# Score maxima of an attention kernel from 28-row bands: two heads by a quarter of the keys in a tile

## The chip, the cores and the metric

One core of one Trainium2 chip. The metric is device time in microseconds (us) of one execution of the whole program; lower is better.

## What is computed

Layer norm of x (2048 rows by 256), cross attention onto a context of 1601 rows with 8 heads of dimension 4, a gated residual, a second layer norm, then a router with 8 experts that each take their 512 best rows:

```
q, k, v = heads(ln(x) @ Wq + bq), heads(ctx @ Wk + bk), heads(ctx @ Wv + bv)
attn = softmax(q @ k.T * scale)              # per head, 2048 x 1601
x = x + tanh(g_x) * (attn @ v @ Wo + bo)
scores = softmax(ln(x) @ router_w + router_b); G, idx = top_k(scores.T, 512)
h1 = relu(toks @ w1 + b1); eo = (h1 @ w2 + b2) * G
x = x + tanh(g_f) * scatter_add(eo, idx)
```

The change is in the attention alone: in how the row maximum of the scores, which the softmax subtracts, is found.

## The kernel before

**Data.** Each number of q and k is split into bf16 parts, so that a head takes 28 rows (partitions) of contraction at most: 6 groups of 4 for the products of the parts, of which rows 24 and 25 also carry the maximum. Four heads stand under each other, head hh at partitions 32·hh to 32·hh+27. qrows holds q in that form (2 groups of 4 heads). kpad (L141) holds k once for each head, with all partitions but the head's own set to zero (L807 and L590 multiply by a 0/1 column), so that a matmul over all 128 partitions gives the scores of one head.

**Units.** The queries go in 4 chunks of 512, times 2 groups of 4 heads: 8 units, numbered u = 0 to 7. A unit has 13 steps (kt), one for each tile of 128 keys (the last has 65). In a step TensorE does, for each head hh of the group:

- a score matmul (L1287, called S here), 128 keys by 512 queries, into bank hh mod 2. It waits until ScalarE has read what was there before, two heads earlier (L1284).
- ScalarE's exponential of it (L609), which writes probs in fp32.
- after the second S of a step, the product of the step before with the values (L1191, called P here): 4 heads, 4 column groups of the array, fp32, 8 records.

**The maximum.** It has to be known before a unit's scores are taken. So it is found one unit ahead, two steps early (LEAD, L295): max_scores (L1165, called M here) makes a tile of two 401-column matmuls (L1175) of 128 queries against kpad, in two neighbouring banks; VectorE reduces the tile (max_half, L811 to L814). Before, both matmuls of a tile are of one head with one stationary block of q, and the tile is that head's half of the keys. A unit has 32 tiles (HALVES, L43). halves_of (L297) spreads them over the steps: 3 in steps 0, 2, 4, 6, 8 and 10 of a unit, 2 in the other seven. On TensorE the order of a step is S M S (M) P S M S, where (M) is there in steps of 3 tiles only. Unit 0's 32 tiles and the first 4 of unit 1 (EARLY, L301) stand ahead of all steps. Unit 7 computes no maxima. max_parts (L816) takes the maximum over a head's tiles, place_max (L1178) and q_full bring it into rows 24 and 25 of qfull.

**Side jobs.** At the end of some steps, behind the fourth S, stands a job of TensorE for a neighbouring chunk (L314 and on): transposes (L1199, L1132, L1206, L1220, L1232), place_max (L1181), the output projection (wo, L1210 to L1214), the q projection (L1138), the router (L1226).

**Loops.** All engines write chunk 0 and chunk 3 out and run chunks 1 and 2 in a loop with a register (on TensorE L1328, ScalarE L655, VectorE L941).

Of the kernel before, what the change touches and what calls it, by code (L numbers as in the profile page):

```python
# [13 lines left out]
ALU = mybir.AluOpType  # L14
ACT = mybir.ActivationFunctionType
AX = mybir.AxisListType

P = 128
# [12 lines left out]
NC = 4  # L31
CT = QT // NC
CW = CT * P
# [3 lines left out]
HG = 4  # L37
# [2 lines left out]
NKB = len(KB) * NG  # L40
MAXW = 401
MAXSTEP = 400
HALVES = CT * HG * 2  # L43
ROW_V = 28
KROW_M = 24
BITS = 30
# [50 lines left out]
def build(nc, x, ctxt, g_x, g_f, Wq, bq, Wk, bk, Wv, bv, Wo, bo, rw, rb, w1, b1, w2, b2, cf, cdigits, out, x2d):  # L97
# [9 lines left out]
    with es:  # L107
# [3 lines left out]
        def sem(name):  # L111
            return es.enter_context(nc.semaphore(name))
# [25 lines left out]
        def ar(name, shape, dt=F32):  # L138
            return arena.enter_context(nc.sbuf_tensor(name, shape, dt))

        kpad = ar("kpad", [P, NH, KEYS], BF16)  # L141
        vp = ar("vp", [P, NKT, NG, HG, 32])
        qrows = ar("qrows", [P, NG, S], BF16)
# [10 lines left out]
        rec = ar("rec", [P, CT, HG])  # L154
        on = ar("on", [P, CT, NG, HG, HD])
        mparts = ar("mparts", [P, CT, HG, 32], BF16)
        mhalf = ar("mhalf", [P, HALVES])
        nmax = ar("nmax", [P, CT * HG])
        wq_sb = ar("wq_sb", [P, KD, 32])
        wk_sb = ar("wk_sb", [P, KD, 32])  # L160
# [74 lines left out]
        ps = es.enter_context(nc.psum_tensor("ps", [P, 8, 512], F32))  # L235
# [18 lines left out]
        s_mm, s_mr, s_nm, s_mhi, s_mp, s_mpl, s_qf = [sem(n) for n in ("max_scores", "max_reduced", "max_negated", "max_high", "max_parts", "max_placed", "q_full")]  # L254
# [19 lines left out]
        s_dn, s_bi, s_eo, s_put = sem("down_steps"), sem("b2_added"), sem("expert_out"), sem("rows_added")  # L274

        block = es.enter_context(nc.Block())

        def kt_rows(kt):
            return P if kt < FULLKT else KREST
# [20 lines left out]

        EARLY = HALVES * LEAD // NKT  # L301
        PLACE = NKT - LEAD
# [399 lines left out]
        def _(dve):  # L702
# [12 lines left out]
            for w, r in ((wk_sb, wkr), (wq_sb, wqr)):  # L715
                for k in range(KD):
                    for g in range(NG):
                        last = nc.vector.tensor_copy(
                            r[:, k, g, :].rearrange("p (h j d) -> p h j d", h=HG, d=HD)[:, :, 0:6, :],
                            w[:, k, 16 * g:16 * g + 16].rearrange("p (h d) -> p h d", d=HD).unsqueeze(2).to_broadcast([P, HG, 6, HD]))  # L720
# [7 lines left out]
            for j in range(2):  # L728
                for g in range(NG):
                    last = nc.vector.tensor_copy(  # L730
                        bqkr[:, NG * j + g, :].rearrange("p (h j d) -> p h j d", h=HG, d=HD)[:, :, 0:6, :],
                        bias_sb[:, 32 * j + 16 * g:32 * j + 16 * g + 16].rearrange("p (h d) -> p h d", d=HD).unsqueeze(2).to_broadcast([1, HG, 6, HD]))
# [67 lines left out]
            for j in range(4):  # L800
                lo, w = KB[j]
# [3 lines left out]
                for hh in range(HG):  # L805
                    last = nc.vector.tensor_scalar(kpad[:, hh, lo:lo + w], krows[:, 0:w],
                                                   cst[:, C_HEAD + hh:C_HEAD + hh + 1], None, ALU.mult)  # L807
# [3 lines left out]
            def max_half(u, j):  # L811
                dve.wait_ge(s_mm, HALVES * u + j + 1)
                b = 2 + 2 * (j % 2)
                nc.vector.tensor_reduce(mhalf[:, j:j + 1], ps[:, b:b + 2, 0:MAXW], AX.XY, ALU.max).then_inc(s_mr, 1)  # L814

            def max_parts(u):  # L816

                dve.wait_ge(s_mr, HALVES * (u + 1))
                nc.vector.tensor_reduce(nmax[:, :], mhalf[:, :].rearrange("p (n h) -> p n h", h=2), AX.X, ALU.max,
                                        negate=True).then_inc(s_nm, 1)  # L820
                dve.wait_ge(s_nm, u + 1)
                at_least(dve, s_mpl, u)
                nm = nmax[:, :].rearrange("p (t h) -> p t h", h=HG)
                nc.vector.tensor_copy(mparts[:, :, :, KROW_M], nm).then_inc(s_mhi, 1)
                dve.wait_ge(s_mhi, u + 1)
                nc.vector.tensor_tensor(mparts[:, :, :, KROW_M + 1], nm, mparts[:, :, :, KROW_M], ALU.subtract).then_inc(s_mp, 1)
# [117 lines left out]
            c = NC - 1  # L944
# [130 lines left out]
            for e in range(E):  # L1075
                for f in range(NF):
                    n = NF * e + f
# [16 lines left out]
                for t in range(NT):  # L1094
                    dve.wait_ge(s_dn, DOWN * e + STEPS_F + 2 * (t // 2) + 2)
                    at_least(dve, s_eo, NT * (e - 1) + t + 1)
                    a = D * (t % 2)
# [4 lines left out]
        def _(pe):  # L1102
            mm = nc.tensor.matmul

            pe.wait_ge(s_wrep, 1)
            for j in range(2 * NG):
                last = mm(job[:, j:j + 1], bqkr[:, j, :], cst[0:1, C_ONE:C_ONE + 1], start=True, stop=True)
# [33 lines left out]
            for j in range(4):  # L1141
                for k in range(KD):
                    n = KD * j + k
                    pe.wait_ge(s_ctx[j], 16)
                    at_least(pe, s_ctt, n - 3)
                    for t in range(4 if j < 3 else 1):
                        w = kt_rows(4 * j + t)
                        last = nc.tensor.transpose(ps[:, n % 4, P * t:P * t + w], ctx_sb[0:w, 4 * j + t, P * k:P * k + P],
                                                   cst[0:w, C_ID:C_ID + w])
# [14 lines left out]

            def max_scores(u, c, g, j):  # L1165

                t, hh, half = j // (2 * HG), (j // 2) % HG, j % 2
                if j == 0:

                    pe.wait_ge(s_rows, ROWS_OF_UNIT[u] if isinstance(u, int) and u < 2 else NKB + u + 1)  # L1170
                at_least(pe, s_mr, HALVES * u + j - 1)
                q = qrows[:, g, bass.ds(CW * c + P * t, P)]
                for b in range(2):
                    lo = MAXSTEP * (2 * half + b)
                    last = mm(ps[:, 2 + 2 * (j % 2) + b, 0:MAXW], q, kpad[:, HG * g + hh, lo:lo + MAXW], start=True, stop=True)  # L1175
                last.then_inc(s_mm, 1)

            def place_max(u):  # L1178
# [146 lines left out]
                return owner[0]  # L1325

            chunk(0, True, False)
            with pe.Fori(1, NC - 1) as i:  # L1328
                chunk(i, False, False)
            owner = chunk(NC - 1, False, True)  # L1330
            c = NC - 1
# [77 lines left out]
            for e in range(E):  # L1409
                for f in range(NF):  # L1410
# [3 lines left out]
                    if f >= LAG:  # L1414
# [3 lines left out]
                        for t in range(NT):  # L1418
                            last = down(e, f - LAG, t)
# [5 lines left out]
                for t in range(NT):  # L1425
                    for f in range(NF - LAG, NF):
                        last = down(e, f, t)
# [21 lines left out]
```

## Time and profile before

| | |
|---|---|
| median of 3 runs | 698.83 us (698.7 to 701.12) |
| the profiled execution | 701.08 us; its span, from the first to the last instruction, 699.3 us |
| mean granted TensorE clock | 0.933 of full speed |
| busy: TensorE matmul, VectorE, ScalarE, GpSimd | 588.2, 479.8, 405.2, 160.4 us |
| projections and unit 0's maxima | to about 75 us |
| the steps of units 0 to 6, with maxima beside them | about 75 to 379 us |
| the steps of unit 7, without | about 379 to 414 us |
| router, search of the thresholds | to about 487 us |
| experts | to the end |

Engine names in the rows: PE is TensorE's matmul, PEld its weight load, DVE is VectorE, ACT is ScalarE, POOL is GpSimd. "128\*32" behind a matmul is rows by columns of the array that it uses. The duration of a PE record is longer than the time for which it holds the next one up: records overlap, so the distance between two starts is what a matmul costs.

### The profile page before, as it was taken

To read this page: it belongs to the slowest core of one execution; us is meant where nothing else is said; L and a number is where in the kernel's file an instruction comes from. 1 tells how busy PE (TensorE), PEld (TensorE's weight loads), DVE (VectorE), ACT (ScalarE), POOL (GpSimd) and SP (SyncE) were. 2 spreads that over 40 slices of the span, in tenths; PEclk is the share of its full clock that TensorE was granted. 3 is DMA by queue.
4 is the path that set the end of the run, shared out by engine and by line. 5 is a ranking of instruction groups with operands and counts; after the bars stand their busy time and mean duration, and the time that the engine had idled before them with its cause. 6 is when DMAs were issued, how large, how long until landed. Compare 5 with 4: busy or idle time off the path is not lost.

```text
span 699.3 us, 10376 instructions
## 1 busy us (share of the span) xinstructions
PE 588.2 (84%) x3452; PEld 318.1 (45%) x3452; DVE 479.8 (69%) x952; ACT 405.2 (58%) x748; POOL 160.4 (23%) x161
## 2 busy tenths in 40 slices
PE   4875899999999999999999983012999999999992
PEld 4421233323333234332332231002889888988991
DVE  3789977779788797886877014885576786786531
ACT  2554478767778677877677961000555666565551
POOL 3023202002030020560000001003143653463333
PEclk9989899999999999999999995555999999999997
DMA  7500000000000000000001005001135554463322
GB/s 249 185 1 0 1 1 0 2 1 1 1 31 31 1 0 0 30 30 0 1 1 60 1 1 180 0 0 38 53 100 141 121 135 126 103 172 100 61 31 30
DMA packets 23326, 35.39 MB, mean 51 GB/s; under 512 B 3411, under 2 KB 15988, under 8 KB 23156
## 3 DMA queue, kind: packets, MB, share of 16 engines
q1 hardware_dynamic: 17140, 26.45, 11.5%
q0 software_dynamic: 6144, 8.39, 7.1%
q8 instruction: 24, 0.39, 0.2%
q14 instruction: 18, 0.15, 0.1%
HBM read 26.45 MB, written 8.39 MB: 50 GB/s over the span
## 4 chain that ended last, share of the span: by engine, by line
PE 71%; DVE 11%; ACT 7%; issue 4%; POOL 2%; DMA 0%; POOLq 0%; DVEq 0%; ACTq 0%
PE ps L1191 14%; PE ps L1392 13%; PE ps L1399 13%; PE ps L1287 13%; PE ps L1175 9%; ACT probs L609 5%; DVE mhalf L814 4%; DVE ge L988 3%; PE ps L1138 2%; PE ps L1214 1%; PE ps L1226 1%; PE ps L1374 1%; PE ps L1115 1%; PE ps L1220 1%; ACT c L540 1%
## 5 line engine op out<-in xcount | busy, mean ns | idle before, releaser
L814 DVE TENSOR_REDUCE mhalf<-ps 128x1 f32<-128x802 f32 x256 | 247.5, 988 | 62.9 <-PE ps L1175 60.4
L609 ACT ACTIVATE probs<-ps 128x512 f32<-128x512 f32 (+1 forms) x416 | 233.1, 599 | 91.0 <-PE ps L1287 88.5
L1287 PE MATMUL ps<-qfull,kpad 128*128 128x512 bf16 (+1 forms) x416 | 153.0, 384 | 7.5 <-ACT probs L609 2.0
L1175 PE MATMUL ps<-kpad,qrows 128*128 128x401 bf16 x512 | 132.8, 343 | 13.2 <-DVE mhalf L814 11.7
L1191 PE MATMUL ps<-probs,vp 128*32 128x512 f32 (+1 forms) x832 | 110.8, 604 | 1.5 <-ACT osb L529 0.9
L1287 PEld LDWEIGHTS ps<-qfull,kpad 128*128 128x128 bf16 (+1 forms) x416 | 40.1, 99 | 141.2 <-ACT probs L609 120.9
L1079 DVE TENSOR_TENSOR h1l<-hf,h1h 128x512 fp32r<-128x512 f32 x64 | 44.5, 695 | 62.3 <-ACT hf L689 54.6
L688 ACT ACTIVATE h1h<-ps,b1T 128x512 fp32r<-128x512 f32 x64 | 43.9, 686 | 60.6 <-PE ps L1392 60.4
L1399 PE MATMUL ps<-w2h,h1h 128*128 128x256 f32 x256 | 73.8, 288 | 3.3 <-issue 2.6
L1175 PEld LDWEIGHTS ps<-kpad,qrows 128*128 128x128 bf16 (+1 forms) x512 | 46.2, 99 | 59.0 <-DVE mhalf L814 27.2
L1399 PE MATMUL ps<-w2l,h1h 128*128 128x256 f32 x256 | 72.4, 283 | 0.0
L1399 PE MATMUL ps<-w2h,h1l 128*128 128x256 f32 x256 | 72.3, 282 | 0.0
L499 POOL DMA_INDIRECT out<-eo,idx_put x32 | 56.9, 1777 | 29.3 <-ACT eo L698 20.2
L413 POOL TENSOR_SCALAR rstd<-mv 128x4 f32<-128x4 f32 x8 | 1.9, 232 | 229.5 <-DVE mv L750 229.5
L1392 PE MATMUL ps<-tokh,w1h 128*128 128x512 f32 x128 | 52.5, 410 | 1.5 <-DVE tokl L1065 1.5
L1399 PEld LDWEIGHTS ps<-w2h,h1h 128*128 128x128 f32 x256 | 48.8, 191 | 7.8 <-issue 5.8
L1392 PE MATMUL ps<-tokl,w1h 128*128 128x512 f32 x128 | 51.1, 399 | 0.0
L1392 PE MATMUL ps<-tokh,w1l 128*128 128x512 f32 x128 | 50.6, 395 | 0.0
L1399 PEld LDWEIGHTS ps<-w2l,h1h 128*128 128x128 f32 x256 | 48.9, 191 | 1.2
L1399 PEld LDWEIGHTS ps<-w2h,h1l 128*128 128x128 f32 x256 | 48.9, 191 | 0.0
L689 ACT ACTIVATE hf<-ps,b1T 128x512 f32<-128x512 f32 x64 | 43.7, 683 | 0.0
L529 ACT ACTIVATE tokh<-ps 128x512 fp32r<-128x512 f32 x16 | 8.8, 601 | 51.9 <-PE ps L1374 51.9
(167 smaller groups left out, 668.6 us busy)
## 6 DMA issues: line engine op xcount, KB each, us to landing
w1raw<-in_L_ffn_w SPq DMA_DIRECT2D x16, 512.0 KB, 4.1
w2raw<-in_L_ffn_w SPq DMA_DIRECT2D x16, 512.0 KB
xs<-in_x SPq DMA_DIRECT2D x4, 512.0 KB, 8.1
out<-xs SPq DMA_DIRECT2D x4, 512.0 KB, 2.7
x_rows<-x SPq DMA_DIRECT2D x4, 512.0 KB, 2.6
ctx_sb<-in_ctx SPq DMA_DIRECT2D x3, 512.0 KB, 6.2
b2b<-in_L_ffn_b SPq DMA_DIRECT2D x1, 1024.0 KB, 12.9
toks<-x_rows,idx_get POOLq DMA_INDIRECT x32
```

What stands on the lines that cost most here:

```text
L499: nc.gpsimd.indirect_dma_start(out=out_rows, out_offset=bass.IndirectOffsetOnAxis(ap=idx_put[:, t:t + 1], axis=0), in_=eo[:, t, :], in_off ...
L609: nc.scalar.activation(probs[0:w, par, hh, :], ps[0:w, score_bank(kt, hh, last_unit), :], ACT.Exp, scale=float(SCALE)).then_inc(s_ex, 1)
L688: nc.scalar.activation(h1h[:, f, :], ps[:, bank, :], ACT.Relu, bias=bias).then_inc(s_hh, 1)
L689: nc.scalar.activation(hf[:, f % 2, :], ps[:, bank, :], ACT.Relu, bias=bias).then_inc(s_hf, 1)
L814: nc.vector.tensor_reduce(mhalf[:, j:j + 1], ps[:, b:b + 2, 0:MAXW], AX.XY, ALU.max).then_inc(s_mr, 1)
L988: last = nc.vector.tensor_scalar(ge[:, v, :], scoreT[:, :], cand[:, v:v + 1].bitcast(F32), None, ALU.is_ge, ALU.add, accum_out=cnt[:, v:v ...
L1079: nc.vector.tensor_tensor(h1l[:, f, :], hf[:, f % 2, :], h1h[:, f, :].bitcast(F32), ALU.subtract).then_inc(s_hl, 1)
L1175: last = mm(ps[:, 2 + 2 * (j % 2) + b, 0:MAXW], q, kpad[:, HG * g + hh, lo:lo + MAXW], start=True, stop=True)
L1191: last = mm(ps[32 * hh:32 * hh + 32, PV, :], vp[0:w, kt, g, hh, :], probs[0:w, par, hh, :], start=(kt == 0), stop=(kt == NKT - 1))
L1287: mm(ps[0:w, score_bank(kt, hh, last_unit), :], kpad[:, HG * g + hh, P * kt:P * kt + w], qfull[:, g, :], start=True, stop=True).then_inc(s ...
L1392: last = mm(ps[:, UP_BANKS[f % 3], :], w[:, k, P * f:P * f + P], r[:, k, :], start=(m == 0), stop=(m == len(terms) - 1))
L1399: last = mm(out_t, h[:, f, P * t:P * t + P], w[:, f, :], start=(f == 0 and m == 0 and t % 2 == 0), stop=(f == NF - 1 and m == 2), skip_gro ...
```

## The change

Each matmul of a tile takes only the 28 partitions of its head, from q and from kpad, and the two matmuls of a tile are of two heads (partitions 0 to 27 and 32 to 59, or 64 to 91 and 96 to 123). A tile is thus 2 heads by a quarter of the keys; their number stays 32 in a unit. The reduction gives one value for each of the two heads, and max_parts takes the maximum over 4 values in place of 2. The score matmuls S still use all 128 rows. TensorE's loop over chunks 1 and 2 is written out; the loops of the other engines stay.

```diff
-HALVES = CT * HG * 2
+QUARTERS = 4
+HALVES = CT * (HG // 2) * QUARTERS
...
-        mhalf = ar("mhalf", [P, HALVES])
+        mquart = ar("mquart", [P, CT * HG, QUARTERS])
...
+        def head_rows(hh):
+            return slice(32 * hh, 32 * hh + ROW_V)
...
-                nc.vector.tensor_reduce(mhalf[:, j:j + 1], ps[:, b:b + 2, 0:MAXW], AX.XY, ALU.max).then_inc(s_mr, 1)
+                n, kq = 2 * (j // QUARTERS), j % QUARTERS
+                nc.vector.tensor_reduce(mquart[:, n:n + 2, kq], ps[:, b:b + 2, 0:MAXW], AX.X, ALU.max).then_inc(s_mr, 1)
...
-                nc.vector.tensor_reduce(nmax[:, :], mhalf[:, :].rearrange("p (n h) -> p n h", h=2), AX.X, ALU.max,
-                                        negate=True).then_inc(s_nm, 1)
+                nc.vector.tensor_reduce(nmax[:, :], mquart[:, :, :], AX.X, ALU.max, negate=True).then_inc(s_nm, 1)
...
-                t, hh, half = j // (2 * HG), (j // 2) % HG, j % 2
+                t, pair, kq = j // (2 * QUARTERS), (j // QUARTERS) % 2, j % QUARTERS
...
-                q = qrows[:, g, bass.ds(CW * c + P * t, P)]
+                lo, a = MAXSTEP * kq, CW * c + P * t
                 for b in range(2):
-                    lo = MAXSTEP * (2 * half + b)
-                    last = mm(ps[:, 2 + 2 * (j % 2) + b, 0:MAXW], q, kpad[:, HG * g + hh, lo:lo + MAXW], start=True, stop=True)
+                    hh = 2 * pair + b
+                    last = mm(ps[:, 2 + 2 * (j % 2) + b, 0:MAXW], qrows[head_rows(hh), g, a:a + P],
+                              kpad[head_rows(hh), HG * g + hh, lo:lo + MAXW], start=True, stop=True)
...
-            with pe.Fori(1, NC - 1) as i:
+            for i in range(1, NC - 1):
                 chunk(i, False, False)
```

## Rows read from the trace of the kernel before

**Rows 1.** The page: busy share and TensorE clock in 40 slices of the span
```profile
PE   4875899999999999999999983012999999999992
...
PEclk9989899999999999999999995555999999999997
```
**Rows 2.** Busy time by stretch; units 1 to 7, a line for each
```profile
core 0: us, PE busy (x) PEld busy (x) DVE busy (x) ACT busy (x) POOL busy (x), PEclk, DMA share, GB/s
116.00:157.00 41.00, 39.29 (x230) 12.07 (x228) 32.51 (x38) 29.64 (x54) 1.03 (x1) 1.00 0.00 1
157.00:203.00 46.00, 45.20 (x258) 16.62 (x256) 37.45 (x60) 34.88 (x62) 8.34 (x8) 1.00 0.03 12
...
379.00:412.00 33.00, 32.13 (x193) 8.97 (x192) 3.26 (x13) 30.50 (x61) 0.00 (x0) 1.00 0.04 17
```
**Rows 3.** The page's costliest groups in the attention
```profile
L814 DVE TENSOR_REDUCE mhalf<-ps 128x1 f32<-128x802 f32 x256 | 247.5, 988 | 62.9 <-PE ps L1175 60.4
L609 ACT ACTIVATE probs<-ps 128x512 f32<-128x512 f32 (+1 forms) x416 | 233.1, 599 | 91.0 <-PE ps L1287 88.5
L1287 PE MATMUL ps<-qfull,kpad 128*128 128x512 bf16 (+1 forms) x416 | 153.0, 384 | 7.5 <-ACT probs L609 2.0
L1175 PE MATMUL ps<-kpad,qrows 128*128 128x401 bf16 x512 | 132.8, 343 | 13.2 <-DVE mhalf L814 11.7
```
**Rows 4.** PE in order of time: two neighbouring steps without a side job
```profile
142.93 1.06 PE L1191 MATMUL ps<-probs,vp 128*32 128x512 f32 x8
143.93 0.39 PE L1287 MATMUL ps<-qfull,kpad 128*128 128x512 bf16 x1
144.16 0.51 PE L1175 MATMUL ps<-kpad,qrows 128*128 128x401 bf16 x2
144.50 0.90 PE L1287 MATMUL ps<-qfull,kpad 128*128 128x512 bf16 x2
145.24 0.51 PE L1175 MATMUL ps<-kpad,qrows 128*128 128x401 bf16 x2
145.58 0.38 PE L1287 MATMUL ps<-qfull,kpad 128*128 128x512 bf16 x1
145.80 0.51 PE L1175 MATMUL ps<-kpad,qrows 128*128 128x401 bf16 x2
146.23 1.06 PE L1191 MATMUL ps<-probs,vp 128*32 128x512 f32 x8
147.23 0.39 PE L1287 MATMUL ps<-qfull,kpad 128*128 128x512 bf16 x1
```
**Rows 5.** PEld and ACT of the same steps, with the waits
```profile
145.01 0.10 PEld L1287 LDWEIGHTS ps<-qfull,kpad 128*128 128x128 bf16 x1 [0.58 <-ACT probs L609]
...
145.57 0.10 PEld L1287 LDWEIGHTS ps<-qfull,kpad 128*128 128x128 bf16 x1 [0.23 <-ACT probs L609]
...
144.36 2.23 ACT L609 ACTIVATE probs<-ps 128x512 f32<-128x512 f32 x4 [0.72 <-PE ps L1287]
```
**Rows 6.** PE in order of time: side jobs (transposes, wo, q projection, place_max)
```profile
173.07 0.38 PE L1287 MATMUL ps<-qfull,kpad 128*128 128x512 bf16 x1
173.29 0.60 PE L1132 MATMUL ps<-cst,xn 128*128 128x128 f32 x4
173.72 0.38 PE L1287 MATMUL ps<-qfull,kpad 128*128 128x512 bf16 x1
...
183.02 0.38 PE L1287 MATMUL ps<-qfull,kpad 128*128 128x512 bf16 x1
183.33 1.12 PE L1214 MATMUL ps<-wo_sb,onT 32*128 32x256 f32 x4
184.39 0.39 PE L1287 MATMUL ps<-qfull,kpad 128*128 128x512 bf16 x1
...
186.83 0.38 PE L1287 MATMUL ps<-qfull,kpad 128*128 128x512 bf16 x1
187.05 1.88 PE L1138 MATMUL ps<-xnT,wqr 128*128 128x512 f32 x4
188.77 0.38 PE L1287 MATMUL ps<-qfull,kpad 128*128 128x512 bf16 x1
...
336.53 0.38 PE L1181 MATMUL ps<-ident_bf,mparts 128*128 128x128 bf16 x4
336.82 0.41 PE L1287 MATMUL ps<-qfull,kpad 128*65 128x512 bf16 x1
```
**Rows 7.** wo's last two records and its last; P's second pass of four
```profile
183.86 0.59 PE L1214 MATMUL ps<-wo_sb,onT 32*128 32x256 f32 x2
...
184.08 0.37 PE L1214 MATMUL ps<-wo_sb,onT 32*128 32x256 f32 x1
...
146.69 0.61 PE L1191 MATMUL ps<-probs,vp 128*32 128x512 f32 x4
```
**Rows 8.** Single records, duration in ns (min/median/max): S behind P, S behind M, wo's first, wo's last two
```profile
L1287 PE MATMUL ps<-qfull,kpad x1: 389/389/389, 147.2 to 147.2; 128*128 128x512 bf16 x1
...
L1287 PE MATMUL ps<-qfull,kpad x1: 377/377/377, 183.0 to 183.0; 128*128 128x512 bf16 x1
...
L1214 PE MATMUL ps<-wo_sb,onT x1: 478/478/478, 183.3 to 183.3; 32*128 32x256 f32 x1
...
L1214 PE MATMUL ps<-wo_sb,onT x2: 374/374/374, 183.9 to 184.1; 32*128 32x256 f32 x2
```
**Rows 9.** Busy time in unit 0's maxima, columns as in rows 2
```profile
40.00:45.00 5.00, 4.76 (x11) 1.90 (x10) 3.57 (x5) 2.14 (x4) 2.31 (x2) 0.50 0.01 2
45.00:50.00 5.00, 3.97 (x20) 1.96 (x18) 4.37 (x6) 3.21 (x9) 0.00 (x0) 0.96 0.00 0
...
60.00:65.00 5.00, 3.12 (x13) 0.82 (x13) 5.00 (x7) 2.37 (x7) 0.00 (x0) 1.00 0.00 0
```
**Rows 10.** PE in order of time, inside the loop: two P, a step of 3 tiles apart
```profile
238.26 1.06 PE L1191 MATMUL ps<-probs,vp 128*32 128x512 f32 x8
...
241.56 0.64 PE L1191 MATMUL ps<-probs,vp 128*32 128x512 f32 x4
```
**Rows 11.** Waits of the whole program: us in total, times, longest us
```profile
PEld ps L1287 <- ACT probs L609: 120.9, 198, 0.9
...
PEld ps L1191 <- issue: 16.3, 50, 0.5
```

## The prediction

> **What bounds the kernel now.** I read the page's slices first: TensorE is busy nine tenths or more over the attention and over the experts [rows 1]. The change touches the attention, so I split that by unit. With maxima beside them, units take 41 to 46 us at 96 to 98% PE; unit 7, without, takes 33 us [rows 2]. The groups show why tiles matter: 512 M matmuls, 133 us of PE [rows 3]. But PE busy is not PE full, since records overlap; so I went to the order of time of two neighbouring steps [rows 4] and took distances between starts. There S is 0.22 us, M 0.34 (two streams of 0.17), P 1.00. A step of 2 tiles repeats after 2.95 us (140.98 to 143.93), one of 3 after 3.30 (143.93 to 147.23).
>
> These steps hold two pieces of slack, and everything depends on which M lies in one. Call the S behind P "third", then M, "fourth", the next step's "first", M, "second". At 144.50 the row counts two S, and the M behind them comes 0.74 us later where 0.43 would do: the weight load of "first" stands until 145.01 for ScalarE's exponential of "third" [rows 4, 5]. Third to first is thus 1.08 us, set by ScalarE, while TensorE's own work in it (0.22 + 0.34 + 0.22) would take 0.79: 0.3 us are free. First to second is 0.56, and there both limits meet: TensorE needs 0.22 + 0.34, and the load of "second" is also released by ScalarE at 145.57 [rows 5]. So an M made shorter gains nothing in such a step, except the third M, between "second" and P, which has nothing beside it. Where a side job of 0.43 us or more stands behind "fourth", third to first is TensorE's.
>
> **The change, part by part.** *Two streams at once.* The two matmuls of a tile use rows 0 to 27 and 32 to 59 (or 64 and 96 up). If they stream together, 0.34 becomes 0.17 us. The trace shows this for columns: P's second pass runs as 4 records within 0.61 us where one alone has 0.59 to 0.60 [rows 3, 7]. For rows there is none. The Trainium skill, page TensorE: Matmul & The Clock Gate, section on packing small matmuls, says that row bands run together too, four of them at 3.07 times the speed; no row here shows it. The sum below rests on P.
>
> *Switching between whole array and bands.* This price can be read. wo has 32 rows: from S to wo is 0.31 us where S to a whole-array job is 0.22 (186.83 to 187.05): 0.09 more. wo's last record starts at 184.08 and streams 0.215 (the distance to the record before it, 183.86), yet the next S starts at 184.39: again 0.09. P shows the same: its second pass starts at 146.69, lasts 0.43, S at 147.23; and M to P is 0.43 less 0.17 for the second stream, 0.26, so 0.09 [rows 4, 6, 7]. Behind a switch the weight load isn't hidden either: S behind P lasts 389 ns against 377 (12 ns, bf16), wo's first record 478 against 374 (104 ns, fp32 in 128 columns) [rows 8]. A band tile has two loads. Bounds: 12 ns once, 104 ns twice. I take 24, two bf16 loads of the same column count as the 12 ns row, the nearest one. The same page of the Trainium skill, section on LDWEIGHTS, gives the columns over 1.2 GHz whatever the rows, 107 ns here; exposed once behind each switch, that would put the sum at +18 us, where the 12 ns row gives the +4 below. The fp32 row agrees with that rule, the bf16 row doesn't, and M is bf16.
>
> M in a band: 0.09 in + 0.024 + 0.17 + 0.09 out + 0.012 for the S behind it = 0.386 us, against 0.345: **0.04 more**, although it streams half as long.
>
> *Where that lands.* Units 0 to 5 have tiles in 13 steps, unit 6 in 11: 89 steps. In each, the M between first and second is on the path: 89 x 0.04. The M between third and fourth is covered by the 0.3 us, but not where a side job follows. Those jobs are the 0.43 us transposes and longer; place_max (0.29) fits the slack [rows 6]. By the code: 4 in unit 0, 1 in unit 1, 8 and 5 in units 2 and 3, 8 and 5 in 4 and 5, 4 in 6: 35. Together 124 x 0.04 = +5.0 us. The exponential of "fourth" moves 0.04 later as well and holds "second" no longer than TensorE does.
>
> The third M: second to P is now 0.65 us (145.58 to 146.23). Afterwards 0.215 + 0.09 + 0.024 + 0.17 + 0.09 = 0.59, for a switch to P was paid already. 7 units x 6 steps x -0.06 = -2.5 us.
>
> *Unit 0's maxima* stand one behind the other and wait for VectorE, a tile each 0.99 us or less [rows 3, 9]; TensorE has room, no switch is on the path, no gain. But TensorE will stand idle longer between tiles. The granted clock in this stretch is 1.00 (2.4 GHz), after 0.50 (1.2 GHz) in the stretch before [rows 9], and no row shows it with so little work. If it stays at 1.2 GHz, the q projection (1.72 us between starts at 2.4 GHz [rows 6]) takes 1.7 more, the projections of k and the first steps some 1.8: bounds 0 and +3.5; I take +1.5.
>
> *VectorE.* Same 802 elements a tile, two results in place of one: 0 taken. Beside steps it is hidden (2.5 x 0.99 in 3.1 us), ahead of them 36 tiles show it: 10 ns each would be 0.4 us. max_parts reads 64 values in place of 32: under 0.1 us. *The loop written out* on TensorE: a step of 3 tiles takes 3.30 us from P to P in unit 1, outside the loop (142.93 to 146.23), and in unit 3, inside it (238.26 to 241.56) [rows 4, 10], so 0; its bounds are -0.5 and +0.5, the longest wait that the sequencer itself shows [rows 11]. Semaphores and order are as before; no wait is added, no DMA moved.
>
> Sum: +5.0 - 2.5 + 1.5 = **+4.0 us**. On the profiled execution that is 701.08 + 4.0 = 705.1; this lies 2.25 us above the median of the runs, so for the median 698.83 + 4.0 = **702.8 us**. With the load bounds: one load of 12 ns gives 124 x 0.03 - 42 x 0.07 = +0.8 (+1.5); 104 once gives 124 x 0.12 = 14.9, + 42 x 0.02 = 0.8, + 1.5: 716.0; 104 twice gives 124 x 0.225 = 27.9, + 42 x 0.124 = 5.2, + 1.5: 733.
>
> **Rivals.** *A, faster: the switch isn't paid.* If 28-row bands in bf16 follow S without the 0.09 us, as M does now, M costs 0.17. Then the third M gives 42 x -0.17 = -7.1; the 21 steps with 0.43 us jobs give 0.13 each (then ScalarE's 1.08 holds), -2.7; the 14 with long jobs (q projection, wo, router) give 2 x 0.17, -4.8; the others nothing, for ScalarE holds both places. 698.8 - 14.6 = 684.2. It decides from a switch below 0.05 us. For it: halved streams on an engine at 97%. Against it: wo, a row band itself, pays 0.09 both ways. 11%.
>
> *B, slower by far: the bands switch but run one behind the other.* Then M is 0.555 us, +0.21: 124 x 0.21 = 26, and the third M +0.1 x 42 = 4.4, with +1.5: 731. Against it: P's columns overlap. 9%.
>
> *C, nothing moves.* Either the matmuls of 28 rows run as whole-array ones (S to M stays 0.22, M 0.34), so the change does nothing but leave rows out, or the 0.04 falls into waits for ScalarE and VectorE that I take for exactly full: 698.8 +- 1.5. 14%.
>
> **How the numbers follow.** A measurement of this kernel can tell about 0.5%, 3.5 us, from no change. My case has 66%; its own range is 699.5 to 717, and because its middle lies at the bound, I give 41 of the 66 to slower by over 0.5% and 25 to within. With B: slower 0.50. C gives 12 to no change and 2 to faster, should waits shorten too: same 0.37. A and those 2: faster 0.13. A and B lie outside the range, which reaches from 693 (a switch at half price) to 717 (one long load).
>
> **What would show it.** M records as 28\*128, their two starts within 0.03 us of each other. S to M 0.31 in place of 0.22, M to the next S 0.26 to 0.28 in place of 0.34. Steps of 2 tiles 2.99 in place of 2.95, of 3 about 3.28 in place of 3.30, steps with a job 0.08 longer; unit 7 as before; VectorE's reduction at 0.99 us. The waits of S's weight loads for ScalarE (120.9 us [rows 11]) barely change. Wrong if S to M stays at 0.22 (A or C), if the two starts lie 0.17 apart (B), or if the clock falls inside the steps, where I have it at 1.00 throughout.

## The result and the profile after

The changed kernel takes 707.46 us (median of 4 runs, 706.02 to 707.8), the kernel before 699.98 us on the same chip (4 runs, 698.7 to 701.33). The ratio is 1.0104, 95% interval 1.0089 to 1.012: slower by 1.04%, 7.5 us. (The 698.83 us of the prediction is the median of the first three of these four runs of before.) The profiled execution of the changed kernel took 706.02 us, its span is 704.2 us, its mean granted clock 0.909 where before had 0.933.

The page's groups of the changed kernel that answer to [rows 3], and its clock line, which answers to [rows 1]:

```profile
L820 DVE TENSOR_REDUCE mquart<-ps 128x2 f32<-128x802 f32 x256 | 247.7, 990 | 68.9 <-PE ps L1180 67.0
L614 ACT ACTIVATE probs<-ps 128x512 f32<-128x512 f32 (+1 forms) x416 | 237.6, 598 | 90.3 <-PE ps L1293 87.8
L1293 PE MATMUL ps<-qfull,kpad 128*128 128x512 bf16 (+1 forms) x416 | 156.9, 393 | 6.3 <-ACT probs L614 2.7
L1180 PE MATMUL ps<-kpad,qrows 28*128 28x401 bf16 x512 | 92.2, 359 | 12.5 <-DVE mquart L820 11.0
...
PEclk9955699999999999999999995555899999999997
```

M's busy time fell from 132.8 to 92.2 us, and yet the kernel is slower: busy time is no measure of what a matmul costs. VectorE's reduction is as it was (990 ns; 988 before). The clock line differs from before in its third to fifth slice (556 where 898 stood), 35 to 88 us, and in its 29th (8 for 9), where the experts begin.

The changed kernel in order of time, PE, the same two steps as [rows 4]:

```profile
143.82 1.07 PE L1197 MATMUL ps<-probs,vp 128*32 128x512 f32 x8
144.82 0.39 PE L1293 MATMUL ps<-qfull,kpad 128*128 128x512 bf16 x1
145.15 0.34 PE L1180 MATMUL ps<-kpad,qrows 28*128 28x401 bf16 x2
145.42 0.87 PE L1293 MATMUL ps<-qfull,kpad 128*128 128x512 bf16 x2
146.22 0.34 PE L1180 MATMUL ps<-kpad,qrows 28*128 28x401 bf16 x2
146.50 0.39 PE L1293 MATMUL ps<-qfull,kpad 128*128 128x512 bf16 x1
146.82 0.34 PE L1180 MATMUL ps<-kpad,qrows 28*128 28x401 bf16 x2
147.10 1.06 PE L1197 MATMUL ps<-probs,vp 128*32 128x512 f32 x8
```

Two M records together last 0.34 us, as long as one of them: they run at once. Their starts in the trace are 3 ns apart (170 before). S to M is 0.31 to 0.33 us (0.22 before), M to the next S 0.27 (0.34). A step of 3 tiles takes 3.28 us from P to P here (143.82 to 147.10; 3.30 before). A step of 2 takes 3.00 (2.96 before). The switch costs what wo and P showed before the change. On TensorE alone a pair of bands saves 0.17 us of streaming and pays 0.21 for two switches and their loads.

Where the span's difference lies is best seen by dividing every trace at five starts. (What e0 to e14 are is told in the next section.) The columns are, in us: (a) to the first reduction of a tile, (b) on to the first S, (c) on to the P of step 3 of unit 0, (d) on to the P of step 12 of unit 6, (e) on to the last S, (f) on to the end. (e) is 30.42 in every kernel here, since unit 7 has no M, and is left out.

| kernel | a | b | c | b + c | d | f | clock |
|---|---|---|---|---|---|---|---|
| before | 34.77 | 40.14 | 11.31 | 51.45 | 294.24 | 288.37 | 0.933 |
| changed | 32.88 | 41.50 | 12.23 | 53.73 | 297.63 | 289.54 | 0.909 |
| e0 changed again | 34.38 | 42.24 | 11.27 | 53.51 | 297.62 | 289.52 | 0.912 |
| e1 all rows | 34.91 | 38.09 | 11.12 | 49.21 | 293.89 | 288.76 | 0.925 |
| e2 bands in front | 34.81 | 41.58 | 11.38 | 52.96 | 293.88 | 287.83 | 0.916 |
| e3 bands in steps | 34.92 | 40.23 | 12.66 | 52.89 | 296.05 | 288.55 | 0.928 |
| e4 one head | 33.02 | 47.80 | 17.97 | 65.77 | 335.63 | 289.87 | 0.886 |
| e5 one head, bands in front | 33.03 | 48.93 | 10.31 | 59.24 | 294.11 | 289.88 | 0.905 |
| e6 one matmul in front | 33.02 | 42.00 | 10.32 | 52.32 | 293.84 | 290.13 | 0.916 |
| e7 order, bands | 33.04 | 40.05 | 11.86 | 51.91 | 294.54 | 290.09 | 0.921 |
| e8 order, all rows | 34.91 | 38.14 | 9.92 | 48.07 | 306.21 | 287.74 | 0.928 |
| e9 changed, weights late | 32.88 | 42.26 | 11.27 | 53.53 | 295.36 | 292.59 | 0.913 |
| e10 changed, weights early | 34.81 | 41.59 | 12.31 | 53.90 | 295.43 | 288.75 | 0.911 |
| e11 before, weights early | 34.59 | 40.05 | 11.28 | 51.33 | 293.30 | 288.55 | 0.931 |
| e12 steps, weights early | 33.03 | 40.26 | 12.65 | 52.91 | 295.46 | 288.55 | 0.929 |
| e13 order, bands, side work first | 33.02 | 40.17 | 12.60 | 52.77 | 284.67 | 289.63 | 0.925 |
| e14 order, all rows, side work first | 34.84 | 40.18 | 10.72 | 50.90 | 297.49 | 288.62 | 0.933 |

(a) is the loading of the inputs. It differs by 1.5 us between the two traces of the changed kernel (32.88 and 34.38) and by 2 over all traces, so it is not an effect of the change. From before to changed, b + c is 2.3 longer, d 3.4 and f 1.2. The forecast had 1.5, 2.5 and 0 for these.

The stretches from 45 us on (columns as in [rows 2]), first of the kernel before, then of the changed one:

```profile
45.00:55.00 10.00, 7.33 (x36) 3.14 (x34) 9.37 (x11) 5.12 (x16) 2.31 (x2) 0.98 0.00 0
55.00:65.00 10.00, 6.68 (x26) 2.17 (x25) 9.39 (x12) 5.76 (x16) 0.62 (x2) 1.00 0.00 0
75.00:85.00 10.00, 8.84 (x46) 2.60 (x44) 9.89 (x21) 6.33 (x12) 1.59 (x3) 0.94 0.01 2
```

```profile
45.00:55.00 10.00, 7.65 (x30) 3.29 (x31) 9.70 (x12) 6.45 (x16) 2.30 (x2) 0.60 0.00 0
55.00:65.00 10.00, 6.52 (x22) 1.39 (x21) 7.89 (x10) 4.14 (x12) 0.62 (x2) 0.67 0.00 0
75.00:85.00 10.00, 9.91 (x42) 2.08 (x42) 8.97 (x20) 5.87 (x11) 1.27 (x2) 0.69 0.01 2
```

TensorE is about as busy by its records, but the granted clock is 0.60 to 0.69 where it was 0.94 to 1.00: most of the time at its lower level, 1.2 GHz. The stretch of 75 to 85 us is the first steps.

And inside the steps the clock fell too. First PE, DVE and POOL of the changed kernel at the start of unit 5, then the busy time around:

```profile
299.47 2.00 DVE L762 TENSOR_SCALAR x<-xs,mv,rstd 128x256 f32 x2
...
300.01 1.31 POOL L466 TENSOR_TENSOR w1l<-w1raw,w1h 128x512 fp32r<-128x512 f32 x1
...
302.43 0.34 PE L1180 MATMUL ps<-kpad,qrows 28*128 28x401 bf16 x2 [0.92 <-DVE mquart L820]
302.70 0.39 PE L1293 MATMUL ps<-qfull,kpad 128*128 128x512 bf16 x1
303.02 1.94 PE L1197 MATMUL ps<-probs,vp 128*32 128x512 f32 x8
```

```profile
300.00:303.00 3.00, 1.99 (x12) 0.57 (x8) 3.00 (x5) 2.17 (x4) 3.00 (x4) 1.00 0.00 0
303.00:306.30 3.30, 3.30 (x14) 0.64 (x14) 2.47 (x4) 1.20 (x2) 3.30 (x5) 0.51 0.40 159
306.30:309.00 2.70, 2.70 (x19) 0.95 (x17) 2.16 (x3) 1.79 (x3) 2.70 (x4) 0.97 0.00 0
```

P takes 1.94 us there in place of 1.06. Before it TensorE had waited 0.92 us for a reduction, which stood on VectorE behind two operations of the layer norm. These took 2.00 us, while GpSimd worked on the expert weights (L462 to L469). The kernel before has the same wait at the same place, and its clock did not fall:

```profile
297.47 2.07 DVE L757 TENSOR_SCALAR x<-xs,mv,rstd 128x256 f32 x2
...
300.50 0.52 PE L1175 MATMUL ps<-kpad,qrows 128*128 128x401 bf16 x2 [1.02 <-DVE mhalf L814]
```

### The profile page after: what moved, and what is told of

It is laid out like the page before. It is cut to its first block, busy times and chain, and to the rows that moved or that the text cites. A ratio compares the mean times of both kernels' runs of the same rounds, so it can differ in the third digit from the quotient of the medians.

```text
span 704.2 us, 10063 instructions
## 1 busy us (share of the span) xinstructions
PE 595.0 (84%) x3452; PEld 303.5 (43%) x3452; DVE 479.4 (68%) x952; ACT 409.7 (58%) x748; POOL 158.6 (23%) x161
## 4 chain that ended last, share of the span: by engine, by line
PE 64%; DVE 14%; ACT 9%; issue 5%; POOL 1%; DMA 0%; POOLq 0%; DVEq 0%; ACTq 0%
PE ps L1293 15%; PE ps L1197 14%; PE ps L1398 10%; PE ps L1405 9%; PE ps L1180 7%; ACT probs L614 5%; DVE mquart L820 4%; DVE ge L993 3%; PE ps L1143 2%; PE ps L1220 1%; ACT eo L703 1%; ACT hf L694 1%; PE ps L1232 1%; DVE tokl L1070 1%; DVE h1l L1084 1%
## 5 line engine op out<-in xcount | busy, mean ns | idle before, releaser
L820 DVE TENSOR_REDUCE mquart<-ps 128x2 f32<-128x802 f32 x256 | 247.7, 990 | 68.9 <-PE ps L1180 67.0
L614 ACT ACTIVATE probs<-ps 128x512 f32<-128x512 f32 (+1 forms) x416 | 237.6, 598 | 90.3 <-PE ps L1293 87.8
L1293 PE MATMUL ps<-qfull,kpad 128*128 128x512 bf16 (+1 forms) x416 | 156.9, 393 | 6.3 <-ACT probs L614 2.7
L1197 PE MATMUL ps<-probs,vp 128*32 128x512 f32 (+1 forms) x832 | 112.5, 613 | 1.5 <-ACT osb L534 0.9
L1293 PEld LDWEIGHTS ps<-qfull,kpad 128*128 128x128 bf16 (+1 forms) x416 | 39.6, 98 | 147.6 <-ACT probs L614 113.1
L1180 PE MATMUL ps<-kpad,qrows 28*128 28x401 bf16 x512 | 92.2, 359 | 12.5 <-DVE mquart L820 11.0
L1180 PEld LDWEIGHTS ps<-kpad,qrows 28*128 28x128 bf16 x512 | 24.2, 92 | 83.0 <-issue 50.3
L1398 PE MATMUL ps<-tokl,w1h 128*128 128x512 f32 x128 | 51.2, 400 | 0.0
```

The costliest lines, as they stand in the source:

```text
L614: nc.scalar.activation(probs[0:w, par, hh, :], ps[0:w, score_bank(kt, hh, last_unit), :], ACT.Exp, scale=float(SCALE)).then_inc(s_ex, 1)
L820: nc.vector.tensor_reduce(mquart[:, n:n + 2, kq], ps[:, b:b + 2, 0:MAXW], AX.X, ALU.max).then_inc(s_mr, 1)
L1180: last = mm(ps[:, 2 + 2 * (j % 2) + b, 0:MAXW], qrows[head_rows(hh), g, a:a + P], kpad[head_rows(hh), HG * g + hh, lo:lo + MAXW], start=Tr ...
L1197: last = mm(ps[32 * hh:32 * hh + 32, PV, :], vp[0:w, kt, g, hh, :], probs[0:w, par, hh, :], start=(kt == 0), stop=(kt == NKT - 1))
L1293: mm(ps[0:w, score_bank(kt, hh, last_unit), :], kpad[:, HG * g + hh, P * kt:P * kt + w], qfull[:, g, :], start=True, stop=True).then_inc(s ...
L1398: last = mm(ps[:, UP_BANKS[f % 3], :], w[:, k, P * f:P * f + P], r[:, k, :], start=(m == 0), stop=(m == len(terms) - 1))
```

## The experiments

Two theories stood against each other. Either **the switches** are the cost, as forecast, and the clock is a detail, or a good part of the 7.5 us is **the clock**, which bands bring down where TensorE already has waits. Each ratio is against the kernel before on the same chip, with its 95% interval.

**e1, e2, e3: the bands taken out, or left in one place.** e1 keeps everything of the change but the rows. e2 has bands only in the 36 tiles ahead of the steps, e3 only beside the steps.

```diff
 e1
-qrows[head_rows(hh), g, a:a + P], kpad[head_rows(hh), HG * g + hh, lo:lo + MAXW]
+qrows[:, g, a:a + P], kpad[:, HG * g + hh, lo:lo + MAXW]
 e2, e3
+rows = head_rows(hh) if bands else slice(0, P)
```

> The changed kernel with all 128 rows in the maximum's matmuls; tiles of two heads by a quarter, the reduction and the written-out loop stay. Theory (array switches and a lower clock, both from the bands): as the kernel before, 700.0 us within 1.0, switch-free steps of 2.95 and 3.30 us, granted clock 0.93. Rival (the new tiles, the two-result reduction or the written-out loop cost the part that the switches don't explain): 703 to 705 us.

> Bands only for the 36 tiles ahead of the steps; the tiles beside the steps use all rows. Theory (clock): the granted clock falls to 1.2 GHz there as in the changed kernel, first reduction to second P of unit 0 about 2.3 us longer than before, nothing in the steps: 702.3 us. Rival (the front costs nothing, what is missing comes from the steps): 700.0 us.

> Bands only beside the steps. Theory: switches +2.1 us by the step times (2.99, 3.27, +0.08 with a side job), clock back at 1.00 in the front, and perhaps one fall of the clock at unit 5's long wait, +1.3: 702.0 to 703.5 us. Rival (all of the loss is in the steps): 707 us.

Measured: e1 700.13 us, ratio 0.9996 (0.9982 to 1.001). e2 701.36, 1.0014 (0.9999 to 1.0028). e3 702.45, 1.0039 (1.002 to 1.0059), each the median of 12 runs. So the quarters, the reduction with two results and the loop written out cost nothing that can be measured. In (d), e1 is 0.35 us under before. e3 against e1 in (d) is 2.16: the price of the switches beside the steps, without a fall of the clock. The two parts add to about +3.7 us (0.14% and 0.39%), the change to +7.5. The rest appears only with both: 1.6 us of it in (d), 297.63 - 296.05, and most of what is left in (f), 289.54 where e2 has 287.83 and e3 288.55.

**e4: bands that can't run at once.** Tile as before (one head, half the keys) and the loop written out, but 28 rows, so both matmuls use the same band.

```diff
-q = qrows[:, g, bass.ds(CW * c + P * t, P)]
+q = qrows[head_rows(hh), g, a:a + P]
-... q, kpad[:, HG * g + hh, lo:lo + MAXW]
+... q, kpad[head_rows(hh), HG * g + hh, lo:lo + MAXW]
```

> Bands of 28 rows everywhere, but a tile is one head by half of the keys as before, so that both matmuls use the same band and can't run together; loop written out. Theory (the two bands of the changed kernel stream together, the switch is paid once a tile): M is 0.17 us longer than in the changed kernel, 0.56 in place of 0.39: on the path 124 times and 42 times for the third tile, +28 us on 707.5: 735 us. Rival (no matter which rows, the third and first place have more slack than I count): under 720 us.

Measured: 750.4 us, 1.0713 (1.068 to 1.0745). e4 in order of time, PE:

```profile
153.08 0.39 PE L1292 MATMUL ps<-qfull,kpad 128*128 128x512 bf16 x1
153.40 0.51 PE L1180 MATMUL ps<-kpad,qrows 28*128 28x401 bf16 x2
153.85 0.70 PE L1292 MATMUL ps<-qfull,kpad 128*128 128x512 bf16 x2
```

S to S across M is 0.77 us where the changed kernel has 0.60 (144.82 to 145.42): the 0.17 of the second stream is back. That is the distance that rival B had (0.555 behind 0.215), so bands gain nothing when both matmuls of a tile take the same one. The price came out above the 735 us that were expected. In the trace, which is of the slowest of the four executions (756.61 us; the others took 747.94 to 752.43), the clock was down as well: at 0.50 from 36.5 to 101.3 us, through the front and the first steps, and for 23.9 us in unit 5. e4's busy time before and in that fall:

```profile
320.00:335.00 15.00, 14.52 (x75) 3.54 (x73) 12.47 (x21) 11.12 (x20) 10.79 (x13) 1.00 0.03 12
...
337.00:360.00 23.00, 23.00 (x72) 4.80 (x66) 10.94 (x14) 8.66 (x15) 5.27 (x6) 0.50 0.06 24
```

The first five steps of unit 5 took 29.9 us there, where before took 17.1.

**e0, e5, e6: the front.** e0 is the changed kernel once more. e5 has the bands of e4 in the front tiles, one matmul behind the other, and all rows beside the steps. e6 has all rows everywhere, but in the front, from the third tile on, a tile has only its first matmul. The maxima of the second head are left out there, so its result is not the kernel's.

```diff
 e5, on top of e4
+rows = head_rows(hh) if bands else slice(0, P)
-q = qrows[head_rows(hh), g, a:a + P]
+q = qrows[rows, g, a:a + P]
 e6, on top of e1
-for b in range(2):
+for b in banks:
...
-max_scores(0, 0, 0, j)
+max_scores(0, 0, 0, j, (0, 1) if j < 2 else (0,))
-max_scores(1, 0, 1, j)
+max_scores(1, 0, 1, j, (0,))
```

> The changed kernel once more, unedited, on the chip that the next runs use and with more executions. The two halves measured apart (bands ahead of the steps +1, bands beside them +2 to +3) leave some 3 us of its loss open. Theory (its clock falls inside the steps in every execution, at unit 5's long wait for VectorE, because the front has already left another phase): again +7 us, mean granted clock 0.909 to 0.912, a fall at unit 5 in the trace. Rival (the first comparison was off): +3.7 us, clock 0.915.

> Ahead of the steps bands of 28 rows, but both matmuls of a tile in the same band, so that they stream as long as before (2 x 0.17 us a tile); beside the steps all rows, tiles of one head as before. What makes the clock fall in the front: if it is the shorter streaming, the clock stays at 0.93 and the time at that of before; if it is the 100 rows left out, 0.915 or lower and 1 us more or worse.

> All rows, but ahead of the steps a tile has only its first matmul (from the third tile on); the second head's maxima there come from old data, so that part of the result is left out. Streaming is halved at full rows. If the shorter streaming makes the clock fall, 0.915 and about +1 us; if the rows do, 0.93 and the time of before.

Measured: e0 707.6 us, 1.011 (1.0089 to 1.013), and the clock falls in its unit 5 again, at 304.4 us for 3.4 us. e5 708.58, 1.0119 (1.0096 to 1.0142). e6 701.95, 1.003 (1.0015 to 1.0045). e5, then e6, in the front:

```profile
45.00:55.00 10.00, 9.11 (x26) 3.12 (x26) 7.04 (x8) 4.81 (x11) 2.30 (x2) 0.50 0.00 0
55.00:65.00 10.00, 8.71 (x22) 2.52 (x20) 6.66 (x8) 3.70 (x11) 0.62 (x2) 0.50 0.00 0
```

```profile
45.00:55.00 10.00, 6.52 (x20) 3.21 (x21) 10.00 (x12) 6.49 (x15) 2.30 (x2) 0.76 0.00 0
55.00:65.00 10.00, 6.09 (x14) 1.58 (x12) 7.85 (x10) 3.72 (x11) 1.27 (x3) 0.67 0.00 0
```

e5's matmuls stream as long as the ones of before, one behind the other, and TensorE is busy for 8.7 to 9.1 of 10 us, and yet the granted clock is 0.50 for 51.2 us on end; (b) is 48.93 against 40.14. e6 halves the streaming and keeps the rows, and its clock lies at 0.67 to 0.76, near that of the changed kernel. So both count: less streaming, and fewer rows at the same streaming, each go with the lower clock. With all rows and both matmuls the clock also falls for a while in the front: e1 has 1.00 and 0.75 in these two stretches. But over the whole front, (b), the nine traces with whole-array tiles there have a mean of 0.80 to 0.85, the five with pairs of bands 0.59 to 0.63, e6 0.66, e4 and e5 0.54 and 0.50. And it isn't a matter of single executions: the mean clock of a whole execution is 0.925 to 0.935 in the 12 of e1, 0.913 to 0.918 in the 12 of e2, which differs from e1 by the bands in front alone, and 0.903 to 0.907 in the 4 of e5. The forecast had only the first ("no row shows it with so little work").

**e9, e10, e11: the weights' work moved.** If the wait ahead of unit 5 brings the clock down, it should stay up where GpSimd's work is elsewhere. e9 has it behind the attention, e10 in unit 1. e11 is the kernel before with the move of e10.

```diff
 e9
-first_weights()
 chunk(NC - 1, True, False)
 rstd(NC - 1, mv2, rstd2, s_mv2, s_ve2, s_rs2)
+first_weights()
 e10, e11
 chunk(0, False, True)
+first_weights()
 with pool.Fori(1, NC - 1) as i:
     chunk(i, False, False)
-first_weights()
```

> The changed kernel with GpSimd's split of expert 0's weights moved behind the attention, so that it no longer runs beside VectorE's layer norm at the start of unit 5; that wait (a step of 3.98 us where 3.25 is usual) should go. Theory (the wait makes the clock fall, which costs 1.5 us more): steps 0 and 1 of unit 5 at 3.25 and 3.44, no fall of the clock there, 2.2 us less than the changed kernel. Rival (the fall comes by itself, wherever the phase has it): 0.7 us less, and a fall elsewhere in the steps.

> The changed kernel with GpSimd's split of expert 0's weights moved the other way, into unit 1, where VectorE has only reductions. (Moved behind the attention it took the fall of the clock in unit 5 away, 2.3 us less in the steps, but gave 4 us back between the last score and the threshold search, beside the last layer norm.) Theory: steps 0 and 1 of unit 5 at 3.25 and 3.44, no fall there, nothing given back later: 2.2 us under the changed kernel, 705.4 us. Rival (the fall moves): a fall at another step and 707 us.

> The kernel before with the same move. It has the long wait of unit 5 (4.15 in place of 3.21 us) but no fall of the clock. Theory: 0.8 us less than before, 699 us. Rival: 2 us less, if its other runs have the fall too.

Measured: e9 707.67 us, 1.0109 (1.0088 to 1.013). e10 704.74, 1.0067 (1.0053 to 1.008). e11 699.15, 0.9989 (0.9978 to 1). In both e9 and e10 the fall is gone and (d) is 295.4, 2.2 to 2.3 under e0. In e10 the layer norm's two operations take 0.73 us in place of 2.00:

```profile
301.63 0.73 DVE L762 TENSOR_SCALAR x<-xs,mv,rstd 128x256 f32 x2
```

e9 gives its gain back behind the last S, (f) 292.59: the weights' work now lies beside the second layer norm. VectorE and GpSimd in e9, then VectorE at the same place in the changed kernel:

```profile
425.99 3.76 DVE L762 TENSOR_SCALAR x<-xs,mv,rstd 128x256 f32<-128x256 f32 x4 [1.54 <-POOL rstd L420]
...
427.03 1.30 POOL L466 TENSOR_TENSOR w1l<-w1raw,w1h 128x512 fp32r<-128x512 f32 x1
```

```profile
429.33 1.38 DVE L762 TENSOR_SCALAR x<-xs,mv,rstd 128x256 f32<-128x256 f32 x4 [1.55 <-POOL rstd L420]
```

3.76 against 1.38 us for the same four operations, beside GpSimd and not. The Trainium skill, page "SBUF — State Buffer", section Terms, says that VectorE and GpSimd arbitrate for one pair of ports, as an exclusive lock. The trace fits that, 3.76 against 1.38 us, but doesn't show that these operations took the pair. That the fall went with the wait is shown by e9 and e10. The wait alone isn't enough, though: the kernel before has a longer one (1.02 us) and e3 the same (0.91; its step there takes 3.97 us, the changed kernel's 3.98), and both keep their clock.

**e7, e8: another order.** If a switch is the price, two tiles should share one. In e7 a step of 3 tiles is P S S M M S S M, one of 2 is P S S M M S S, with bands beside the steps; e8 is the same order with all rows. (In the trace the third M runs ahead of the next P.)

```diff
-if hh == 1 and len(halves) == 2:
+if hh == 1 and len(halves) == 3:
     half(*halves.pop(0))
...
-elif hh in (0, 2) and halves:
-    half(*halves.pop(0))
```

> Two tiles one behind the other, behind the fourth score of a step, the third (in steps of 3) behind the second; bands beside the steps, all rows ahead of them. Two tiles share one pair of switches, and no tile stands between first and second. By the rows: steps of 2 tiles 2.91, of 3 tiles 3.19, steps with a side job 0.14 less than before: 9 us less than before, 691 us. Rival (VectorE's two pairs of banks make the second tile wait, or ScalarE sets the step): 698 us or more.

> The same order with all rows everywhere. By the rows: steps of 2 tiles 2.91, of 3 tiles 3.25, with a side job as before: 2 to 3 us less than before, 697.5 us. The difference to the same order with bands is then what bands are worth where a switch is shared: 6 us. Rival (the order alone makes the gain): both the same.

Measured: e7 703.24 us, 1.0062 (1.004 to 1.0083). e8 711.51, 1.0171 (1.0148 to 1.0193). A step of 2 tiles is 2.89 us in both (2.96 before), one of 3 is 3.25 in e7 and 3.48 in e8. That should have made e7 faster than before. What ate it stands in the order of time of a step with the q projection, 6.25 us long where before has 4.71, four of them in the program:

```profile
192.71 0.35 PE L1181 MATMUL ps<-kpad,qrows 28*128 28x401 bf16 x4
...
193.09 1.00 DVE L820 TENSOR_REDUCE mquart<-ps 128x2 f32<-128x802 f32 x1 [1.70 <-PE ps L1181]
194.00 0.74 DVE L854 SCALAR_TENSOR_TENSOR xs<-ps,tg,xs 128x512 f32 x1
194.80 1.98 PE L1143 MATMUL ps<-xnT,wqr 128*128 128x512 f32 x4 [1.74 <-DVE xs L854]
```

The tiles come later in a step, so the reduction that VectorE takes first is late. Behind it stands the residual (L854), and TensorE waits for that with the q projection: 1.74 us. Step 1 of unit 5 is long too, 5.75 us where before has 3.52. e8 has the same long steps (6.38 and 5.65).

**e12, e13, e14: the best version.** e12 is e3 with the weights in unit 1. e13 is e7 with them there, and with VectorE's side work of a step ahead of its reduction. e14 is e13 with all rows.

```diff
 e13, e14, on top of e7 or e8 and of the move in e10
 for at in range(3):
+    beside(i, g, u, (kt, at), first, last)
     if at < len(halves):
         ...
-    beside(i, g, u, (kt, at), first, last)
```

> Bands beside the steps, all rows ahead of them, GpSimd's weight split in unit 1. Theory (switches 2.1 us, front's clock 2.5 us, unit 5's wait and fall 2.9 us; only the first is left): 2.1 us above the kernel before with the same move (0.9 under before), so before +1.2 us; the changed kernel with the move, +4.7, keeps the front. Rival (falls of the clock beside the steps cost more): before +3 us or more.

> Two tiles behind the fourth score and bands beside the steps as in e7, with VectorE's side work put ahead of its reduction and the weight split in unit 1. e7 lost 1.5 us in each of four q projection steps and 2.3 us in unit 5; without: 8.5 us under e7, 694.5 us, 5 to 6 us under before. Rival (the reduction, now later, holds the tiles instead): no better than 700 us.

> The same with all rows. Steps of 2 tiles 2.89, of 3 tiles 3.48 as in e8, side jobs not hidden: 8 us above the one with bands, 702.5 us. Rival (the order and the mending make the gain, not the bands): the same as with bands.

Measured: e12 703.61 us, 1.0049 (1.0032 to 1.0065). e13 **693.15**, 0.9912 (0.9891 to 0.9933), faster than both kernels. e14 703.8, 1.0056 (1.0037 to 1.0075). In e12, (d) is 2.16 over e11, the switches again; but (c) is 1.4 over too, since the clock rose later, at 81.4 us, in the first steps. The same late rise is in e3, at 83.3:

```profile
75.00:85.00 10.00, 9.80 (x38) 1.99 (x39) 8.49 (x18) 5.55 (x10) 1.27 (x2) 0.59 0.01 2
```

PE in order of time of a step of 3 tiles, first e13, then e14:

```profile
141.43 1.06 PE L1198 MATMUL ps<-probs,vp 128*32 128x512 f32 x8
142.42 0.61 PE L1294 MATMUL ps<-qfull,kpad 128*128 128x512 bf16 x2
142.96 0.52 PE L1181 MATMUL ps<-kpad,qrows 28*128 28x401 bf16 x4
143.50 0.88 PE L1294 MATMUL ps<-qfull,kpad 128*128 128x512 bf16 x2
144.40 0.34 PE L1181 MATMUL ps<-kpad,qrows 28*128 28x401 bf16 x2
144.67 1.06 PE L1198 MATMUL ps<-probs,vp 128*32 128x512 f32 x8
```

```profile
143.19 1.06 PE L1198 MATMUL ps<-probs,vp 128*32 128x512 f32 x8
144.19 0.61 PE L1294 MATMUL ps<-qfull,kpad 128*128 128x512 bf16 x2
144.63 0.84 PE L1181 MATMUL ps<-kpad,qrows 128*128 128x401 bf16 x4
145.31 0.83 PE L1294 MATMUL ps<-qfull,kpad 128*128 128x512 bf16 x2
146.22 0.51 PE L1181 MATMUL ps<-kpad,qrows 128*128 128x401 bf16 x2
146.67 0.64 PE L1198 MATMUL ps<-probs,vp 128*32 128x512 f32 x4
```

3.24 against 3.48 us. With the pair of tiles in between, it is 0.85 us from the start of the second S to that of the next in e13 (0.31 and 0.54) and 0.90 in e14: two tiles behind one switch gain 0.05, where one tile alone lost 0.04. The third M starts 0.27 ahead of P where it was 0.45, because P needs a switch anyway: 0.18 more. The steps with the q projection are back at 4.4 to 4.6 us, and those with wo take 3.2 and 3.6 with bands, 3.8 without. Together (d) is 12.8 us shorter with bands than without in this order; the medians differ by 10.6.

## Why the prediction was wrong

It forecast +4.0 us and slower by over 0.5% as the likeliest case. It came out at +7.5, inside the range and with the right sign, but the sum was little more than half of it. The switches were sized right. What failed is the clock, which the sum let act only in the front.

**Two at once, the switch, the loads: right.** The starts lie 3 ns apart (forecast: under 0.03 us), S to M 0.31 (0.31), M to S 0.27 (0.26 to 0.28). This also settles the rule on weight loads that the prediction weighed. The Trainium skill, page "TensorE: Matmul & The Clock Gate", section LDWEIGHTS, gives a load as its columns over 1.2 GHz, 107 ns here; exposed once in each band tile, that estimate made the sum +18 us. The records of M's loads are near it (90 ns in the steps), but (d) of e3 shows +2.16 us for all switches: what a bf16 load adds behind a switch is far less than its own duration. M to the next S, 0.27 us, leaves room for the 12 ns that the prediction took.

**Where it lands: right.** Steps of 2 tiles 3.00 us (2.99), of 3 tiles 3.27 (3.28), steps with a 0.43 us job longer by 0.08 (3.17 against 3.09), unit 7 the same. The sum of +5.0 and -2.5 was +2.5; e3 against e1 and e12 against e11 both give +2.16. ScalarE's hold on S's loads barely changed (113.1 us, 120.9 before [rows 11]).

**The loop at 0: right** within its bounds. e1, which has the loop written out and the new tiles, is at -0.35 in (d). **VectorE at 0: right.**

**The front at +1.5: right in kind, its size open.** b + c grew by 2.1 (e0) to 2.3, within the bounds of 0 to 3.5. Taken against e1, which has the same code but for the rows, it is 4.3 to 4.5: in e1 the clock was at 1.00 from 32.7 to 60.0 us and low from there to 73.7, where before had its low stretches at 38.6 to 45.4 and 69.3 to 76.1. The medians of e2 and e1 put the term at 0.0014 - (-0.0004) of the time, 1.3 us. So how large it is depends on where in the front the clock happens to fall and rise.

**The clock in the steps "at 1.00 throughout": this step failed.** The prediction let the clock act only ahead of the steps. It fell in unit 5, +1.6 us in (d), in both traces of the changed kernel. It also came up late in the first steps: step 1 of unit 0 takes 4.14 us in place of 3.40.

**Behind the steps, taken as nothing: a term that was missing.** The last difference, f, is 1.2 us, in code that the change doesn't touch. There the clock falls once the steps have ended, 4.5 us behind the last S in the changed kernel (both traces), 4.6 in e13, and f is 289.5 to 289.6 in all three; it falls 6.6 us behind it in the kernel before, and 6.6 to 7.5 in e1, e3, e10, e11, e12 and e14, with f from 288.4 to 288.8. But in e2, e6, e7 and e8 it falls at 5.6 to 5.9, and f is anything from 287.7 to 290.1. What f does follow is the moment when the clock comes back for the experts. That is 80.7 and 80.9 us behind the last S in e8 and e2 (f 287.7 and 287.8), 81.7 in the kernel before (288.4), 83.0 in both traces of the changed kernel (289.5), 84.1 and 84.4 in e7 and e6 (290.1). What is left behind that moment is 205.8 to 207.3 us in all traces. In part the experts themselves begin later (77.1 us behind the last S in e2 and e8, 78.3 to 78.5 in the changed kernel, e6 and e7), in part the clock takes longer to rise once they run (3.6 to 3.7 us, 4.6 to 4.7, 5.7 to 6.0). It isn't an effect of bands alone, since e10 has them everywhere and 288.75; what decides it isn't settled.

Added up for e0 against before, in the spans: loading -0.4, front 2.1, steps 3.4 (loop -0.35, switches 2.15, fall 1.6), end 1.15: 6.2 of 6.2 us. The medians say +7.5 and +7.9. The difference lies in which executions were profiled: the one of before took 701.08 us, 1.1 above its median of 699.98, the one of e0 707.35, 0.25 below its own. Against the forecast's 4.0, in these spans, that is 0.6 more in front, 0.9 more in the steps (the fall's 1.6, less 0.35 for the loop and 0.35 for switches) and 1.15 behind them, less 0.4 of loading. The size that the prediction missed by is thus mostly the clock: its fall inside the steps, which is shown by e9 and e10, and its late return for the experts, whose cause stays open.

**The rivals.** A (no switch) and B (serial bands) are excluded by the records; e4 shows what B would have been in the steps. C (nothing moves) is excluded by S to M and by e3. None of them had the clock as the mechanism, and there should have been one: the prediction itself noted that no row showed the clock with so little work in TensorE.

**Left open.** Why the clock falls at unit 5 in the changed kernel and not in e3, which has the same steps, the same weights' work and no fall; what decides when the clock comes back for the experts, and with it (f); and whether e13 would gain from starting the steps at the full clock (its first step takes 4.72 us where e14's takes 3.48). No run here settles these.

## What to carry to other kernels

Row bands save streaming but not time as long as whole-array matmuls stand between them: here a pair of bands saves 0.17 us and two switches with their loads cost 0.21. Put banded work where a switch is paid already (ahead of another tiled matmul, 0.18 us a time here) and put several tiles behind one switch. After such a change of order, look for the engine whose side work now stands behind a later result. And read the granted clock of each stage beside the busy shares, for a matmul on fewer rows may lower it where TensorE has waits already.

## What was unexpected of the hardware

- The granted clock went with the rows used, not with busy time alone. With 28-row matmuls, one behind the other, that streamed as long as whole-array ones, it was 0.50 for 51 us (e5), where whole-array matmuls had 0.98 and 1.00 (before) or 1.00 and 0.75 (e1) from 45 to 65 us. The busy share doesn't show it: it was higher in e5 (87 to 91%, before 67 to 73%), since records last longer at the lower level.
- It can fall amid the steps, after one wait of 0.92 us, and stay down for 3.4 us (changed kernel, e0), or not fall after the same wait (e3, 0.91 us). In e4 it stayed down for 23.9 us at 100% busy PE.
- Two 28-row matmuls of 401 columns start 3 ns apart and both last 0.34 us, so a band's second stream is free. The Trainium skill, "TensorE: Matmul & The Clock Gate", section on packing small matmuls, gives about 4 ns.
- A TENSOR_SCALAR of VectorE on 128x256 fp32 took 2.7 times as long beside GpSimd's casts and subtractions (3.76 against 1.38 us for four). At unit 5 that reached TensorE through VectorE's queue, as a wait of 0.92 us.
